# The edge sort of a two-layer graph network: one-hots column by column, codes from the scalar engine

## What is computed

```python
xn = _layernorm(x)
agg = segment_sum(edge_weight[:, None] * xn[src], dst, num_segments=6250)
x = x + relu(agg @ W + b) + linear_attention(xn)          # layer 0
x = x + experts0(_layernorm(x))
xn = _layernorm(x)
# layer 1: attention over the edges, summed by src and not by dst
e = leaky_relu(h_l[src] + h_r[dst]); att = exp(e - max_by_src) / sum_by_src
x = x + segment_sum(att * h[dst], src, 6250) + mix1(xn)
x = x + experts1(_layernorm(x))
```

## Time and profile before

| | us |
|---|---|
| median of 3 runs | 4306.62 (4291.44 to 4314.83) |
| the profiled execution's own time | 4298.71 |
| its span, first to last instruction | 4297.0 |
| sort stretch, first one-hot to last sort product | 885.6 to 1557.2 |

### The profile page before, as it was taken

One profiled execution on the slowest core, in us unless ns is written; L12 is line 12 of the kernel. 1 busy time (PEld: TensorE's weight loads), 2 busy tenths in 40 slices (PEclk: granted clock), 3 DMA queues, 4 the chain that ended last, 5 costly groups with the idle time before them and its releaser, 6 DMA issues. The chain is left out here.

```text
span 4297.0 us, 46245 instructions
## 1 busy us (share of the span) xinstructions
PE 2891.0 (67%) x12954; PEld 2092.4 (49%) x12954; DVE 2664.2 (62%) x6067; ACT 970.2 (23%) x2628; POOL 2312.0 (54%) x2155
## 2 busy tenths in 40 slices
PE   3456777589999963284665556655656545799986
PEld 2334434355555543163554444434434434699952
DVE  4435898688788784546655556655656576544436
ACT  4565000000000012012321111111111123333332
POOL 0256777766666634254157777777777720365510
PEclk7777887789999875587777677777777765799975
DMA  3322333322232221364123333333333353222233
GB/s 116 83 81 86 88 88 89 91 80 86 83 87 86 83 61 50 71 149 103 62 69 94 92 92 91 92 93 93 93 93 91 92 104 120 74 72 70 72 90 120
DMA packets 203997, 379.28 MB, mean 88 GB/s; under 512 B 48927, under 2 KB 131874, under 8 KB 203620
## 3 DMA queue, kind: packets, MB, share of 16 engines
q0 software_dynamic: 102192, 279.12, 24.1%
q1 hardware_dynamic: 101556, 97.19, 7.3%
HBM read 314.12 MB, written 62.05 MB: 88 GB/s over the span
## 5 line engine op out<-in xcount | busy, mean ns | idle before, releaser
L516 POOL DMA_INDIRECT arena<-h_table,arena x1712 | 1867.0, 1091 | 926.0 <-issue 487.7
L530 DVE TENSOR_TENSOR arena<-arena,ps 128x260 f32 (+1 forms) x1712 | 720.8, 421 | 789.6 <-remote 306.0
L2131 PE MATMUL ps<-arena 128*128 128x260 f32 x1760 | 603.8, 492 | 241.1 <-issue 117.7
L1174 PE MATMUL ps<-arena 128*128 128x256 f32 x1664 | 550.3, 447 | 226.1 <-DVE arena L530 113.5
L2131 PEld LDWEIGHTS ps<-arena 128*128 128x128 f32 x1760 | 394.6, 242 | 359.4 <-issue 236.4
L1174 PEld LDWEIGHTS ps<-arena 128*128 128x128 f32 x1664 | 334.4, 221 | 392.9 <-issue 220.7
L1099 PE MATMUL ps<-arena 128*128 128x224 f16 x784 | 293.9, 528 | 49.5 <-DVE arena L942 48.1
L2113 PE MATMUL ps<-arena 128*128 x880 | 126.0, 188 | 267.3 <-ACT arena L1976 154.3
L843 DVE TENSOR_SCALAR arena<-arena 128x128 f32<-128x128 f32 x832 | 289.2, 348 | 0.4 <-DVE arena L857 0.2
L2058 DVE TENSOR_TENSOR arena<-arena 128x1024 f32<-128x1024 f32 x220 | 268.3, 1220 | 2.1 <-ACT arena L1984 2.1
L2457 POOL DMA_INDIRECT arena<-xn_table,arena x114 | 124.4, 1091 | 250.1 <-POOLq L2188 213.9
(11 more groups left out here) (516 smaller groups left out, 4535.5 us busy)
## 6 DMA issues: line engine op xcount, KB each, us to landing
arena<-h_table,arena POOLq DMA_INDIRECT x1712
arena<-in_L_ffn_w SPq DMA_DIRECT2D x32, 512.0 KB, 7.3
xn_table<-arena SPq DMA_DIRECT2D x14, 896.0 KB
slot_out<-arena SPq DMA_DIRECT2D x21, 512.0 KB
arena<-y_rows SPq DMA_DIRECT2D x12, 896.0 KB, 9.3
h_table<-arena SPq DMA_DIRECT2D x7, 924.0 KB
h_table<-arena SPq DMA_DIRECT2D x7, 896.0 KB, 4.1
arena<-in_x SPq DMA_DIRECT2D x48, 128.0 KB
```

The costliest lines, as they stand in the source:

```text
L516: pool.indirect_dma_start(slot[:, 0:width], None, table, bass.IndirectOffsetOnAxis(ap=idx, axis=0)).then_inc(done, 16)
L530: dve.tensor_tensor(to, to, bank(b, width), ALU.add).then_inc(gnn_add, 1)
L1174: pe.matmul(bank(n % V0_BANKS, D), hot_w[:, g % 2, u, :], rows[:, n % RING, :], start=True, stop=True).then_inc(gnn_ps, 1)
L2131: pe.matmul(bank(4 + u % GNN1_BANKS, ACC_W), hot[:, b, u, :], rows[r][:, u, 0:ACC_W], start=True, stop=True).then_inc(gnn_ps, 1)
```

## The change

The one-hots of the slots are laid column by column and have two buffers, which take the place of `tot_s` and `base_s`, free by then. Their step no longer has a product behind it: steps 0 and 1 raise a new semaphore, `slots_made`, and ACT makes the codes, at the place in its program of the same visit: 14 activations per sort group (7 columns, 2 codes), each 112 elements with the edge's code as scale, one value per partition, from float32 arrays (`code_f`) in place of the fp16 ones. ACT waits for the slots and for the products of two sort groups before. The codes of one column lie next to each other. DVE's step 1 waits for ACT's codes of two sort groups before. PE takes a sort group four visits after the place of the former step 2, not two; that place stays empty on DVE. `hot_pos` is as before, with the column innermost.

```diff
+        slots_made = sem("slots_made")
...
-        slots_ = take(SLOTS_S * GS // 2).bitcast(F16).rearrange("p (n c) -> p n c", c=GS)
-        codes = [take(SLOTS_S * GS).bitcast(F16).rearrange("p (k n c) -> p k n c", k=2, c=GS) for _ in range(2)]
+        iota_n = take(SLOTS_S // 2).bitcast(F16)
+        codes = [take(SLOTS_S * GS).bitcast(F16).rearrange("p (c k n) -> p c k n", c=GS, k=2) for _ in range(2)]
...
-        code_16 = eq_s[:, 0:2 * half_c].bitcast(F16).rearrange("p (k c) -> p k c", k=2)
+        code_f = [scan_s[:, 0:2 * half_c], eq_s[:, 0:2 * half_c]]
...
+        slots_ = [a[:, 0:SLOTS_S * GS // 2].bitcast(F16).rearrange("p (c n) -> p c n", c=GS) for a in (tot_s, base_s)]
...
-        KEYS_AT = MID + 3
+        KEYS_AT, SORT_LAG = MID + 3, 4
...
-            o = sort_op(g - (u < 2), (u - 2) % U)
+            o = sort_op(g - (u < SORT_LAG), (u - SORT_LAG) % U)
...
+                def give_codes(sg):
+                    b = sg % 2
+                    act.wait_ge(slots_made, 2 * sg + 2)
+                    if sg >= 2:
+                        act.wait_ge(sort_ps, sg - 1)
+                    for c in range(GS):
+                        for k in range(2):
+                            at = sg * GS + c
+                            last = act.activation(codes[b][:, c, k, :], slots_[b][:, c, :], ACT.Copy,
+                                                  scale=code_f[k][:, at:at + 1])
+                    last.then_inc(sort_in, 1)
...
                     for u in range(U):
+                        o = sort_op(g, u)
+                        if o is not None and o % 3 == 1:
+                            give_codes(o // 3)
...
-                        V.then(dve.memset(code_16, 0.0))
+                        for a in code_f:
+                            V.then(dve.memset(a, 0.0))
...
-                        V.then(dve.tensor_copy(code_16[:, 0, 0:C], b[:, 0:C]))
+                        V.then(dve.tensor_copy(code_f[0][:, 0:C], b[:, 0:C]))
...
-                        V.then(dve.tensor_scalar(code_16[:, 1, 0:C], a[:, 0:C], 1.0, None, ALU.add))
+                        V.then(dve.tensor_scalar(code_f[1][:, 0:C], a[:, 0:C], 1.0, None, ALU.add))
                     else:
+                        V.add(dve.tensor_copy(iota_n, iota[:, 0:SLOTS_S]))
...
-                        V.add(dve.tensor_tensor(hot_pos[sg % 2], iota_c,
-                                                lane_16[:, at].unsqueeze(1).to_broadcast([P, P, GS]), ALU.is_equal))
+                        dve.tensor_tensor(hot_pos[sg % 2], iota_c, lane_16[:, at].unsqueeze(1).to_broadcast([P, P, GS]),
+                                          ALU.is_equal).then_inc(slots_made, 1)
                     elif step == 1:
-                        V.add(dve.tensor_tensor(slots_, iota_c[:, 0:SLOTS_S, :],
-                                                slot_16[:, at].unsqueeze(1).to_broadcast([P, SLOTS_S, GS]), ALU.is_equal))
-                    else:
-                        V.settle()
-                        dve.tensor_tensor(codes[sg % 2], slots_.unsqueeze(1).to_broadcast([P, 2, SLOTS_S, GS]),
-                                          code_16[:, :, at].unsqueeze(2).to_broadcast([P, 2, SLOTS_S, GS]), ALU.mult
-                                          ).then_inc(sort_in, 1)
+                        if sg >= 2:
+                            dve.wait_ge(sort_in, sg - 1)
+                        dve.tensor_tensor(slots_[sg % 2], iota_n.unsqueeze(1).to_broadcast([P, GS, SLOTS_S]),
+                                          slot_16[:, at].unsqueeze(2).to_broadcast([P, GS, SLOTS_S]), ALU.is_equal
+                                          ).then_inc(slots_made, 1)
...
                         last = pe.matmul(bank(5, 2 * SLOTS_S), hot_pos[sg % 2][:, :, c],
-                                         codes[sg % 2].rearrange("p k n c -> p (k n) c")[:, :, c],
+                                         codes[sg % 2][:, c, :, :].rearrange("p k n -> p (k n)"),
                                          start=(n == 0 and c == 0), stop=(n == PER_PART - 1 and c == GS - 1),
                                          skip_group_check=True)
```

## The result

The changed kernel takes 4250.65 us (median of 4 runs, 4246.08 to 4251.6) against 4300.02 for the kernel before (4 runs, 4291.44 to 4314.83): a ratio of 0.988 with an interval of 0.9855 to 0.991, so faster by 49 us where 106 had been forecast from the median (102 from the profile). It lies inside the range and close to its upper end. Spans: 4249.9 us for 4297.0.

A forecast was written before the change was run, and what follows sets the result against it. PE was taken to bound the gather loop beside the edge sort; 385 visits going from 1.744 to 1.48 us gain 102 us, so 4298.7 becomes 4197, plus 4 toward the runs' median: 4201 us, range 4163 to 4262.

The forecast's parts named there:

- PE's part: Sort matmuls: pitch 0.35 to 0.13 us, a group of seven 2.63 to 1.05 us, PE 1.62 to 1.16 us per visit.
- DVE's part: Sort stretch: code product removed (1.09 us a group), slots one-hot dearer by 0.34; DVE 1.40 to 1.18 us per visit.
- ACT's part: Sort stretch: fourteen activations per group, 0.37 us each, 4.0 us a group; ACT carries 1.31 us per visit.
- Rival C: Sort matmuls: strided weights set the pitch, which stays 0.35 us; 4299 to 4307 us, chance 0.05.
- D: Fourteen activations: ACT becomes the bound at 0.37 us pitch (25 us slower) or 0.39 (60); 4324 to 4366 us, chance 0.07.
- POOL's part and the sum: Sort stretch: POOL's own pace 1.41 us per visit, 1.48 taken for 1.744 over 385 visits, gaining 102 us.
- the signs that I named: Sort stretch: record prices; 344 gathers in some 510 us, POOL's PE wait a fifth, PE about 80% busy, clock below 0.90.
- A: The forecast case: POOL sets the sort stretch's pace, 1.41 to 1.55 us per visit; 4165 to 4232 us, chance 0.70.
- Rival B: Sort stretch: ACT's codes come late and PE waits; pace 1.62 us per visit, 4251 to 4259 us, chance 0.12.

The follow-up runs named there:

- run 6: Kernel before with only the new layout of slots and codes, DVE still making the codes, lag 2: 3998.11 us, ratio 0.9956.
- run 7: Changed kernel with codes laid as before, so ACT writes and PE reads them seven elements apart, lag 4: 4103.74 us, ratio 1.0216.
- run 1: Changed kernel with the sort products taken two visits after step 2's place, not four: 4385.73 us, ratio 1.0099.
- run 9: The changed kernel measured again, no edit: 4284.44 us, ratio 0.9892 to the kernel before.
- run 2: Changed kernel with three buffers, not two, for hot_pos, slots and codes, lag still four: 4278.82 us, ratio 0.9853.
- run 3: Changed kernel with three buffers for hot_pos, slots and codes, products taken six visits later: 4281.86 us, ratio 0.9866.
- run 4: Changed kernel with a constant as scale of ACT's fourteen activations, edge codes left out; only the sort stretch is read: 4457.06 us, ratio 1.0279.
- run 11: Changed kernel with three buffers and lag six, POOL still up to 16 gathers ahead: 4271.16 us, ratio 0.9854.
- run 12: Changed kernel with three buffers, lag six and POOL held to 8 gathers ahead, not 16: 4270.11 us, ratio 0.9847.
- run 5: Changed kernel with POOL held to 8 gathers ahead of the products, not 16, in layer 0's loop: 3893.26 us, ratio 0.9699.
- second comparison: One of three sets of runs, each with its own runs of the kernel before, which took 4014.31 us in this one.

## Why the forecast was right in direction and half right in size

**Which part was right.** PE's part: I took 0.13 us per product and 1.05 per group; they measured 0.107 and 0.90, PE 430/375 = 1.15 us per visit for the 1.16 forecast. That the pitch was set by the moving operand's stride and not by the weights' is shown from both sides: run 6 has the short record (295 ns) with DVE's codes, run 7 the long one again (528 ns) with ACT's; the strided weights are in all of them. DVE's part: slots 0.967 (0.96 forecast), DVE 449/375 = 1.20 per visit (1.18). ACT's part: 0.375 (0.37) and 14 in 4.03 (4.0), ACT 1.27 per visit (1.31). Rival C is out, and so is D for this kernel: ACT is at 79%. "ScalarE: Activation LUTs" in the Trainium skill, section "Rules for kernel authors", would have kept the product on VectorE; its threefold advantage is stated for bf16 operations with one source, and this product has two. By the traces VectorE is indeed the faster per group (1.09 us against 4.03) and that did not decide here: run 6, which keeps the product there, gains 0.4% and no more, and run 7 makes the same move to ACT with another write stride and loses 2%.

**The step that failed** is "POOL's part and the sum": the pace of 1.48. The gather itself came out shorter than I had put it, 1.036 us for 1.112; with issue, 100.2/375 = 0.27, POOL's own pace was 1.30 and not 1.41. (The 0.30 of issue took in 4.9 us of waits for PE: the earlier trace rows has 66.8 us of issue over 235, 0.28.) What I had wrong was the wait: I put 0.07 us per visit over POOL's own pace (1.48 - 1.41), because both neighbour stretches had so little. It was 0.30. 1.036 + 0.267 + 0.301 = 1.60. Hence 385 x (1.744 - 1.600) = 55 us for 102. Of the signs that I named, those on prices held, and those on the pace did not: 344 gathers took 550 us, not 510; POOL's wait did not fall to a fifth; PE is 72% busy, not 80; the granted clock is 0.91, not below 0.90. The time missed A's own 4165 to 4232, to which I gave 0.70, and lies in the range only because the range takes in B. (In D a pitch of 0.39 us makes some 50 us and not 60: 13 x 0.39 + 0.46 = 5.5 us a group, 1.74 of work, a pace of 1.87. It changes nothing.)

**Rival B gave the number (1.62, 4251 to 4259) and not the cause.** It said that PE waits for late codes. They are late sometimes, 53.8 us of PE's time, and lag 2 shows that it can decide (run 1). But at lag 4 it no longer does: with three buffers and lag 6 the codes are there (7.9 us), with a constant scale they are there and PE waits 2.7 us for them, and the pace stays at 1.60 to 1.65. That B's number came out is luck.

**What the wait is made of, as far as shown.** POOL waits for PE when the ring is full of rows that nobody has multiplied. In every run with stops and a lag of four or six, POOL waits about as long, 0.30 to 0.37 us per visit: 113 us (changed), 124 (run 9), 121 (run 2), 125 (run 3), 117 (run 4), 135 (run 11), 129 (run 12), each as "PE" plus "remote" over 600 us. In run 5, with no stop in the trace, it was 17.7 us of 300, 0.08 per visit, near to the 0.07 that I had forecast, even though there POOL is held sooner. So the missing gain goes with the stops. How one becomes POOL's wait is what the timeline shows from 1358 to 1368. How much of the 113 us they make is not shown: late updates end 16 of POOL's 64 waits and account for 19.7 us in them, and the rest would have to come by way of a PE, DVE and ACT held up earlier. (The kernel before waited 0.36 per visit with no stops there, with PE at 93%; I read it so that this wait went, as forecast, and the other is in its place.) DVE, ACT and PE stand together because updates that they wait for, PE's nearly all, come late; why these come late stays open. It isn't ACT's lateness or load (runs 3, 4) nor how far POOL runs ahead (run 12). The kernel before has such waits too, in its stretch 200 to 400 (DVE's add, 37.2 us, 9 times, to 7.1), where ACT is busy with other activations (49 of PE's 113 updates late), but none in its sort stretch. A busy ACT is not enough, as run 1 has ACT 69% busy and few late updates. My guess was the loading of instructions, since ACT's rose from 134 to 1673 in the stretch. The trace speaks against it. It has rows of instruction packets: from 900 to 1200 queue q14's rose from 11 to 18, but run 5 has 20 and no stops, and in the longest stop only one packet was read, in 1.2 us. And DVE, ACT and PE each went on within 0.04 us of the late update that they waited for. One more rival is untested, the recording itself: the traces with late updates also lack updates (589 recorded of 668 that PE's products make in the stretch), while run 5's trace lacks none (633 of 633).

**How large the gain is without the stops** was not measured, since the changed kernel itself did not run in the second comparison. Run 5, which differs from it in the ring alone, has 0.970 there, and the forecast of 102 us in 4307 is 0.976. As the ring made no difference in run 12, I read 0.970 as the gain where nothing stops; that is argued, not shown. With no late update the forecast's mechanism comes out: in run 5 a gather is 1.033, its issue 59.8/216 = 0.277 and POOL's wait 0.082, together 1.39, with ACT (91%) the fullest engine.

**Both halves are needed**: layout alone 0.9956, ACT alone 1.0216, both with lag 2 1.0099, both with lag 4 0.988 and 0.989. (The first two come from the second comparison, where no stops were and both together, with the ring at eight, had 0.970.) "ACT alone" carries the price of its strided writes, so it isn't the worth of DVE's relief by itself.

## What to carry to other kernels

Look first at how the moving operand of a matmul lies: a stride of 14 bytes cost three times the pitch here (0.35 us for 0.107), while the weights kept their stride in every run, and its price, if any, lay beside the products. When work is moved to an idle, slower engine, give its consumer the lag that it needs (2 visits lose 1%, 4 win 1.2%) and check the write stride of the slower engine. Don't take a neighbour stretch's pace for what a stretch will reach once its bound is gone: that stretch has another mix of engines, and the range must reach to the present waits staying as they are. When a wait's releaser ended long before, look whether the semaphore's update came late before blaming the engine that waits.

## What the runs showed of the hardware, expected or not

- An activation of 112 fp16 elements takes 0.375 us with its output contiguous and 0.875 us with the output elements 14 bytes apart (runs 9 and 7).
- A per-partition scale costs 375 - 283 = 92 ns more than a constant (runs 9 and 4), as forecast from the copies of the earlier trace rows (91).
- A weight load of 128 columns takes 0.13 us with its columns 14 bytes apart, and seven of them (0.68 us) lie wholly beside seven products (0.90 us; the changed kernel at 1102.82).
- The semaphore updates of PE's products can come up to 6.5 us after the product, several together, so that DVE, ACT and PE stand, for 5.8 us at the longest in the changed kernel, while POOL goes on. DVE's waits of this kind come 13 times in its 600 us and 29 in run 11's. This came with a time of the kernel before of 4300 to 4337 us and was absent at 4014 us, where no update of PE's was over 0.02 us late. The gathers' pace in the stretch 250 to 400 went with it, 1.47 and 1.29 us per visit (changed kernel and run 7); that of 450 to 800 did not (236 and 238 gathers).
